# First row transposes and first up product ahead of the last positions and counts; the seventh group's shared down tiles behind the last block; POOL's second copies behind the y scatters

## The reference, cut to what matters

```python
x = x + jnp.tanh(g_xattn[0]) * _L0_xattn_ref(_layernorm(x, axis=-1), ctx_1024)
x = x + jnp.tanh(g_ffn[0]) * _L0_ffn_ref(_layernorm(x, axis=-1), shared_w1, shared_w2, experts_w1, experts_w2, gate_w)
...
    shared = jnp.einsum('td,dh->th', x_flat, shared_w1.T)
    shared = jnp.einsum('th,hd->td', jax.nn.silu(shared), shared_w2.T)
    gate_logits = x_flat @ gate_w.T
    top_k_gates, top_k_idx = jax.lax.top_k(gate_logits, TOP_K)
    top_k_gates = jax.nn.softmax(top_k_gates, axis=1)
...
    selected = jnp.einsum('ted,te->td', expert_out, gates)
    return (shared + selected).reshape(B, S, D)
```

## Time and profile before

| what | us |
|---|---|
| median of 3 runs | 233.18 |
| lowest and highest | 233.11, 234.87 |
| the profiled execution | 234.53 |
| its span, first to last instruction | 232.8 |
| PE busy in it | 223.9 |
| POOL busy in it | 160.3 |
| ACT busy in it | 133.4 |
| DVE busy in it | 117.8 |

### The profile page before, as it was taken

One profiled execution on the slowest core, in us unless ns is written; L12 is line 12 of the kernel. 1 busy time (PEld: TensorE's weight loads), 2 busy tenths in 40 slices (PEclk: granted clock), 3 DMA queues, 4 the chain that ended last, 5 costly groups with the idle time before them and its releaser, 6 DMA issues.

```text
span 232.8 us, 6020 instructions
## 1 busy us (share of the span) xinstructions
PE 223.9 (96%) x1664; PEld 197.2 (85%) x1666; DVE 117.8 (51%) x546; ACT 133.4 (57%) x304; POOL 160.3 (69%) x232
## 2 busy tenths in 40 slices
PE   7999999999999699999999999999999999999990
PEld 3975867695677499999999999999999999999870
DVE  6899998866864558499330232202220222178203
ACT  2667896597566306556556655565556555566530
POOL 4762886887777777777777887778776444567620
PEclk9999999999999979999999999999999999999999
DMA  6999110111145687777667665676877667799653
GB/s 234 257 424 350 41 52 31 51 54 51 52 136 158 157 197 196 187 195 183 172 173 197 188 177 156 197 208 195 251 248 217 200 214 229 221 327 387 212 171 121
DMA packets 30463, 43.47 MB, mean 187 GB/s; under 512 B 5232, under 2 KB 16752, under 8 KB 30176
## 3 DMA queue, kind: packets, MB, share of 16 engines
q1 hardware_dynamic: 25248, 32.87, 48.8%
q0 software_dynamic: 4320, 9.41, 11.4%
q10 hardware_dynamic: 864, 0.80, 1.0%
HBM read 30.45 MB, written 12.62 MB: 185 GB/s over the span
## 4 chain that ended last, share of the span: by engine, by line
PE 86%; DMA 8%; DVE 1%; SPq 1%; issue 1%; POOL 1%; ACT 1%; DVEq 0%; POOLq 0%; ACTq 0%
PE bank L1306 27%; PE bank L1329 27%; PE bank L1159 11%; PE bank L1147 10%; PE bank L1280 4%; DMA kT<-in_ctxT 4%; PE bank L1096 2%; DMA xres<-in_xP 2%; DMA nT<-y_rows 1%; PE bank L1103 1%; PE bank L1111 1%; DMA y_rows<-y,dest 1%; PE bank L1086 1%; SPq L339 1%; POOL y_rows L543 1%
## 5 line engine op out<-in xcount | busy, mean ns | idle before, releaser
L543 POOL DMA_INDIRECT y_rows<-y,dest x71 | 71.8, 1011 | 32.8 <-ACT y L720 20.9
L512 POOL DMA_INDIRECT expert_rows<-n,slot x64 | 62.8, 982 | 22.7 <-issue 11.6
L1329 PE MATMUL bank<-w,hT 128*128 x568 | 74.5, 275 | 0.0
L1306 PE MATMUL bank<-xT,w_ring 128*128 128x128 f32 (+1 forms) x432 | 73.9, 308 | 0.0
L1329 PEld LDWEIGHTS bank<-w,hT 128*128 128x128 f32 x568 | 71.3, 192 | 1.6
L714 ACT ACTIVATE hT<-bank 128x512 f32<-128x512 f32 x71 | 42.4, 597 | 40.6 <-PE bank L1306 39.6
L1306 PEld LDWEIGHTS bank<-xT,w_ring 128*128 128x128 f32 x432 | 59.3, 192 | 1.8
L1014 DVE COPY xT<-bank 128x512 f32<-128x512 f32 (+2 forms) x19 | 12.4, 654 | 77.9 <-PE bank L1280 77.9
L720 ACT ACTIVATE y<-bank,gate 128x128 f32<-128x128 f32 x71 | 26.1, 367 | 21.3 <-PE bank L1329 20.9
L1159 PEld LDWEIGHTS bank<-sw,sT 128*128 128x128 f32 x224 | 28.9, 199 | 5.5 <-issue 5.2
L1159 PE MATMUL bank<-sw,sT 128*128 128x128 f32 x224 | 30.3, 284 | 0.0
(11 more groups left out here) (153 smaller groups left out, 211.8 us busy)
## 6 DMA issues: line engine op xcount, KB each, us to landing
w_ring<-in_w1T SPq DMA_DIRECT2D x54, 256.0 KB, 3.5
x_ring<-expert_rows SPq DMA_DIRECT2D x71, 72.5 KB, 3.1
w<-in_w2T SPq DMA_DIRECT2D x2, 1024.0 KB, 11.9
kT<-y_rows SPq DMA_DIRECT2D x8, 256.0 KB, 6.9
nT<-y_rows SPq DMA_DIRECT2D x7, 256.0 KB, 4.2
out<-xres SPq DMA_DIRECT2D x7, 256.0 KB
kT<-in_ctxT SPq DMA_DIRECT2D x3, 512.0 KB, 6.3
xres<-in_xP SPq DMA_DIRECT2D x3, 512.0 KB, 7.7
```

The lines of the kernel that those rows point to most:

```text
L512: pool.indirect_dma_start(out=x_dram[:, :], out_offset=bass.IndirectOffsetOnAxis(ap=slot[:, i, k:k + 1], axis=0), in_=n[:, i, :], in_offse ...
L543: pool.indirect_dma_start(out=y_dram[:, :], out_offset=bass.IndirectOffsetOnAxis(ap=dest[:, b:b + 1], axis=0), in_=y[:, j], in_offset=None ...
L1306: last = pe.matmul(ps_up(b)[:, j * width:(j + 1) * width], w1_ring[:, w % W_RING, c * P:(c + 1) * P], xT[:, s % X_SETS, i * P:i * P + widt ...
L1329: last = pe.matmul(ps_y(b), hidden(b, c), w2[:, ds(at + c * D, D)], start=(c == 0), stop=(c == HC - 1))
```

## The change

```diff
-    AHEAD_OF_BLOCKS = 6
+    LATE = LAST - 1
...
-        ps_so, ps_sup = [bank[4], bank[7]] * (GROUPS // 2), [bank[5], bank[6]]
-        ps_last_sup, ps_last_so = [bank[1], bank[2], bank[5], bank[6]], [bank[0], bank[1]]
+        ps_so, ps_sup = [bank[4], bank[7]] * (LATE // 2) + [bank[0]], [bank[5], bank[6]]
+        ps_last_sup, ps_last_so = [bank[1], bank[2], bank[5], bank[6]], [bank[1], bank[2]]
...
                 if b == COMBINE_AT:
-                    sp.wait_ge(shared_done, LAST)
+                    sp.wait_ge(shared_done, LATE)
...
-            pool.wait_ge(slots_done, GROUPS + 1)
-            for g, t in later[:AHEAD_OF_BLOCKS]:
-                scatter_x(g, t, 1)
             for b in range(USED):
                 scatter_y(b)
-                if b < len(later) - AHEAD_OF_BLOCKS:
-                    g, t = later[b + AHEAD_OF_BLOCKS]
+                if b == 0:
+                    pool.wait_ge(slots_done, GROUPS + 1)
+                if b < len(later):
+                    g, t = later[b]
                     scatter_x(g, t, 1)
...
             silu(0)
-            copy_shared(LAST - 1)
             silu(1)
...
+            choose(LAST)
+            copy_xT(0)
+            place(LAST)
+            gate_gaps(0)
+            copy_xT(1)
             count_rows()
+            gate_gaps(1)
             place_second()
+            early_rows()
+            tables_full()
+            region_ends()
...
+            def add_late_shared():
+                dve.wait_ge(late_summed, 1)
+                dve.wait_ge(sdown_done, LATE + 1)
+                dve.scalar_tensor_tensor(out=xres[:, group(LATE)], in0=ps_so[LATE][:, :], scalar=tanh_g[:, 1:2],
+                                         in1=xres[:, group(LATE)], op0=ALU.mult, op1=ALU.add).then_inc(out_done, 1)
...
             for g in range(GB, GROUPS):
                 add_first(g)
-            for g in range(GB, LAST):
+            for g in range(GB, LATE):
                 add_second(g)
+            add_late()
             add_last_half(0)
             add_last_half(1)
+            add_late_shared()
             add_last_shared(0)
             add_last_shared(1)
...
-                elif bank_of(b, Y_BANKS) == 7:
-                    pe.wait_ge(shared_out, LAST - 1)
                 else:
-                    pe.wait_ge(shared_out, LAST)
+                    pe.wait_ge(shared_out, LATE)
...
             pe.wait_ge(xT_done, SETS)
+            for t in range(G):
+                shared_down(LATE, t)
```

## The result

The changed kernel takes 235.46 us in the median of 17 runs, the kernel before 234.41 us on the same chips (233.18 in the three runs shown ahead). The ratio is 1.0056, 95% interval 1.0031 to 1.0082: 1.3 us longer. That is less than the 1% named ahead as the limit of a measurement; with this many runs the interval still leaves 1 out. The forecast was 3.9 us longer, 237.1 us. The sign and the place were right; the size was not.

The account below looks back on a forecast made before the run. PE was taken to bound the kernel, with set 9's rows, held by POOL's order, deciding the change. Set 9 late 1.5, half clock 1.7 and tail 0.7 made 3.9 us on 233.18: 237.1 us, range 233.8 to 239.3.

Parts of the forecast that it names:

- the wait and its place: SP's wait ahead of set 9's loads grows from 0.7 to over 8 us; PE's only long gap after 90 us there.
- set 9 late by 1.5 us: At set 9's fourth transpose: 16 y scatters ahead of the last second copy make its rows land 1.5 us later than before.
- The sum: Set 9's chain: last second copy issued 134.0, SP's wait ends 137.2, last load issued 140.5, landing 143.6, needed at 142.17.
- The rule of the Trainium skill: For the scatter and row load at set 9: 2.2 us each, set 9 0.4 us earlier than before, total 235.2.
- half clock behind set 9, 1.7 us: After PE's wait of 4 to 6 us at set 9 the clock drops, costing 1.7 us; bounds nothing and 2.2.
- the tail, 0.7 us: Behind the last y scatter: group 6's PSUM sum now stands ahead of the last two, 0.7 us; bounds nothing and 1.5.
- the second rival: Little change: set 9 late but at a small price, by quick landings or full clock; 235.4 us, chance 15%.

Follow-up runs that it names:

- the added traffic of ACT: The changed kernel with twelve more 256 KB loads from ACT's queue behind blocks 23 to 27, into unused tiles; 1.0415 of the kernel before.
- the second copies two later: The changed kernel with POOL's second copies starting two y scatters later; 1.0222 of the kernel before.
- the weights behind the wait: The changed kernel with two 256 KB weight loads between the end of SP's wait and set 9's row loads; 1.0239 of the kernel before.

## Why the prediction was right and wrong

**Right: the wait and its place.** SP's wait is 9.8 us (over 8 forecast), the last second copy goes at 135.11 (134 forecast, 0.9 of the difference being this execution's later front), PE waits for rows at set 9 alone after 90 us, set 2's transposes come between 82.68 and 85.69 (84 to 86), and most of the early gain is spent at set 9. With POOL's old order 1.8 us come back.

**Wrong: the term "set 9 late by 1.5 us".** The step that failed is the time from the last copy's issue to the landing of set 9's last row load. The sum had 9.6 us for it (126.42 to 132.96, and 3.1); in the changed kernel it was 7.2 (135.11 to 142.3). Set 9's last transpose ends 67.6 us behind SP's first row load, where it ended 68.3 us behind it before: 0.7 us earlier and not 1.5 later. When a transfer has landed is told by the updates of its semaphore in the trace, 16 for a row load. By them the difference, 2.5 us before rounding, is made of three parts:

- *The last row load's landing, 1.2 us.* The sum had 3.1 us. It was 1.9 us in the changed kernel (issued at 140.38), and it was 1.9 already in the profile that the sum was made from (issued at 132.96). The earlier trace rows doesn't speak for 71 loads: of these the view has a landing for six only, those issued at 79.03, 100.48, 124.31, 144.38, 164.83 and 187.57. The last five are each the first of a set's four, behind weight loads in SP's queue. By the updates the first of four takes 3.0 us in the median of sets 3 to 17 of that profile and the last of four 2.1 (1.8 to 4.2), and what counts at set 9 is the last.
- *The last copy's landing, 1.0 us.* It took 3.3 us before and 2.3 in the changed kernel. Here the wait that holds SP helps: the DMA engines are busy 0.79 of that time before and 0.18 in the changed kernel.
- *The four issues, 0.3 us.* From the first to the last issue it is 2.75 us before, where one issue took 0.60, and 2.44 in the changed kernel.

One of each kind, both in a busy stretch: the load issued at 124.31 in the kernel before, first of its four, and the one issued at 125.44 in the changed kernel, last of its four, with the DMA engines busy 0.62 of the time until it landed (columns as in the earlier trace rows):

```profile
DMA to landing us min/median/max: 3.5/3.5/3.5
```

```profile
DMA to landing us min/median/max: 2.0/2.0/2.0
125.44:127.48 2.04, 2.04 (x17) 1.94 (x17) 1.25 (x5) 0.85 (x2) 1.48 (x2) 1.00 0.62 161
```

Set 9's four loads landed after 3.0 us (the first) down to 1.9 (the last) in the kernel before and after 1.8, 1.8, 1.8 and 1.9 in the changed one; while the last one was under way the DMA engines were busy 0.49 of the time before and 0.46 in the changed kernel. So quieter engines aren't the reason that the deciding load was quicker than the sum had it: it had been as quick before. With 1.9 in place of 3.1 the prediction's own chain makes set 9 0.3 us late, and with the copy's 2.3 it isn't late at all. The rule of the Trainium skill that was weighed there ("DMA: Bandwidth & Descriptors", section "Anatomy of one DMA": 2.0 us and the bytes, 2.2 here by estimate) is given for transfers issued from GpSimd, so it bears on the copy and not on SP's load. For the copy it is near the 2.3 us of the changed kernel, and far off where the added traffic of ACT kept the DMA engines busy 0.91 of the time: 5.2.

**Wrong: the term "half clock behind set 9, 1.7 us".** PE came at 140.4 (139.5 without this execution's later front), at the late end of the 137.7 to 139.4 forecast, and its rows came at 142.3, not 143.6. The wait was 1.1 us in two pieces between transposes, where 4 to 6 us were forecast, and the clock stayed full (PEclk of the page; it had been low earlier, behind set 2). Behind longer waits there the term came: behind 2.47 us in the second copies two later, and behind 1.76 us in the weights behind the wait.

**Right: the tail, 0.7 us.** From set 10 (149.33 before, 149.90 after) to the end it is 84.2 us against 83.5. The cause given was half of it: PE's last tiles bind as well. The prediction called them hidden, although its own figures have them done at 230.95 at the latest and asked for at 230.8.

**Luck.** The measured 235.46 us lies next to the 235.4 of the second rival. But the kernel before took 234.41 in the same measurement, not 233.18; the rise is 1.3 us, where that rival had 2.2. It had quick landings and full clock as alternatives, and both came.

**Not seen: the execution that the sum was made against.** The three terms as measured, against the profile ahead, are -0.7, 0 and +0.7: nothing. Yet 1.3 us are there in the medians. The profile ahead was of an execution with half clock from 82.14 to 85.55. Of 52 executions of the kernel before 30 had a mean clock of 0.996 or more and a median span of 231.7 us, the other 22 one of 233.05. The changed kernel has 233.7 in either case, as it would if what the half clock takes away ahead of block 28 is waited for there anyway. Against the execution without half clock set 9 is 0.9 and 0.3 us late (67.6 and 67.0 against 66.7), and with the tail (84.2 and 84.4 against 83.5) that makes 1.6 and 1.2 us; against those with it (68.2 in the mean) it makes 0.1 and -0.3. The 1.3 us of the medians lie between. I had read the half clock as part of the kernel, and the 1.7 us as room that any new order could earn; a lower mean clock is there in 22 of 52 executions, and of the three that were profiled two have it at this place. The page "TensorE: Matmul & The Clock Gate" of the Trainium skill (section "Part 1: The HAM clock gate") says that the monitor behind the clock runs freely and doesn't start with the kernel, so that the same gap may fall differently in it. That agrees with two executions that have the same gap of 1.0 us ahead of set 0 and not the same clock behind it; that this is the cause isn't shown by them.

**Still open.** By the median spans the changed kernel is 2.0 us longer than executions without half clock and 0.65 longer than those with it, 0.4 to 0.9 us more on either side than the profiles account for. These are three profiles of the kernel before and two of the changed one, and their fronts differ by 0.9 us ahead of SP's first row load (74.09 to 75.06 in one and the same kernel), so a difference of this size isn't settled by them. Nor does a lower mean clock go with a longer span everywhere: with POOL's old order in the changed kernel the median span is 232.7 us for the five executions at 0.996 or more and 231.8 for the seven below, which nothing here explains. Whether the first row load behind weight loads is slow because of the queue or because of the engines wasn't separated either.

## What to carry to other kernels

An edit that lets the bound engine run ahead is worth what the next queue can follow: look in every other engine's list for what has been put behind something else, and add up its chain from the last fixed point to the use. Take the durations of that chain from the very transfers in it, at their place in their queue, and look at how many transfers a median rests on before you use it. A wait that holds a queue can also leave the DMA engines quieter for the others: the last copy landed 1.0 us earlier for it. And before a stall or a low clock is counted as room, look at whether it is there in every execution.

## What the runs showed of the hardware

A row load of 72.5 KB that was the last of four in SP's queue landed 1.9 to 2.0 us after its issue with the DMA engines busy 0.46, 0.49 and 0.62 of the time. Behind two weight loads of the same queue the first of four took 3.0 us at 0.67 (set 9 of the kernel before); over sets 3 to 17 of that profile the medians are 3.0 us for the first and 2.1 for the last. With twelve loads of 256 KB from another engine's queue beside it, at 1.02, a row load took 5.9. GpSimd's last copy landed after 2.3 us at 0.18, 3.3 at 0.79 and 5.2 at 0.91. The same gap of PE, 1.0 us ahead of set 0 with two shorter ones before it, was followed by half clock for 3.4 us in two of the three profiled executions of one and the same kernel and not in the third; 1.35 us lies between the median span of its 22 executions with a mean clock below 0.996 and that of the other 30.
